# Moving one multiplication from VectorE to GpSimd, pooling the PSUM banks and reordering a four-layer kernel

## The reference

```
num_re = cumsum(p_w * cos(phi)); num_im = cumsum(p_w * sin(phi))
out_re = sum_m(s_re * qr + s_im * qi)
```

## Time and profile before

| what | value |
|---|---|
| median of three runs | 1407.12 us (1404.32, 1407.12, 1527.14) |
| profiled execution | span 1405.9 us; no other time of this execution is listed |
| granted TensorE clock, mean | 0.936 of full speed |
| busy share of the span, PE / DVE / ACT / POOL | 87% / 77% / 75% / 24% |
| HBM traffic | 71 GB/s over the span |

### The profile page before, as it was taken

How to read it: one execution, slowest core, us unless ns; L and a number is a source line. 1 busy time by engine, 2 the same in 40 slices (tenths; PEclk the granted TensorE clock), 3 DMA queues, 4 the chain that set the end, 5 groups by cost and what they waited for, 6 DMA issues and landing times.

```text
span 1405.9 us, 23146 instructions
## 1 busy us (share of the span) xinstructions
PE 1216.6 (87%) x8060; PEld 778.2 (55%) x8060; DVE 1089.1 (77%) x2259; ACT 1052.2 (75%) x2103; POOL 333.9 (24%) x317
## 2 busy tenths in 40 slices
PE   5889885999899988998799989999899988977347
PEld 2575653465556754675556755666566655534224
DVE  3683388788788979889788989898688988887830
ACT  4675788797959878797859888788949887458522
POOL 3944110520133102320124112310133110510101
PEclk9799996999999999999999999999999999998669
DMA  8504141514142123521333041523151140031100
GB/s 254 113 9 102 27 130 42 115 31 116 46 102 72 23 75 88 126 46 41 98 91 82 24 128 28 132 44 103 38 120 38 26 131 28 23 96 50 37 0 15
DMA packets 72084, 101.65 MB, mean 72 GB/s; under 512 B 10640, under 2 KB 44064, under 8 KB 71968
## 3 DMA queue, kind: packets, MB, share of 16 engines
q1 hardware_dynamic: 71968, 100.16, 27.3%
HBM read 74.44 MB, written 25.69 MB: 71 GB/s over the span
## 4 chain that ended last, share of the span: by engine, by line
PE 54%; DVE 16%; ACT 16%; issue 6%; POOL 5%; SPq 1%; DMA 1%; POOLq 0%; DVEq 0%; ACTq 0%
PE ps L873 19%; PE ps L883 15%; PE ps L956 5%; DVE work L1516 4%; ACT work L1203 4%; PE ps L1042 4%; DVE work L1439 3%; PE ps L974 3%; PE ps L948 3%; ACT work L1210 3%; DVE work L1507 2%; ACT xnd L1146 2%; DVE work L1525 2%; PE ps L865 1%; DVE work L1394 1%
## 5 line engine op out<-in xcount | busy, mean ns | idle before, releaser
L1516 DVE TENSOR_TENSOR_SCAN work<-work 128x512 f32<-128x512 f32 x256 | 313.1, 1255 | 39.5 <-ACT work L1270 37.8
L1203 ACT ACTIVATE work<-work 128x384 f32<-128x384 f32 (+3 forms) x512 | 264.4, 559 | 54.6 <-DVE work L1439 52.7
L1439 DVE CUSTOM_DVE_ANT_0 work<-ps,work 128x384 f32<-128x384 f32 (+3 forms) x512 | 228.0, 486 | 90.8 <-PE ps L948 87.0
L752 POOL TENSOR_TENSOR later_norms<-later_norms,singles 128x2 f32<-128x2 f32 x112 | 97.0, 867 | 768.9 <-ACT xnd L1146 465.4
L956 PE MATMUL ps<-ident,work 128*128 128x128 f32 x1280 | 203.4, 285 | 21.4 <-DVE work L1439 10.2
L956 PEld LDWEIGHTS ps<-ident,work 128*128 128x128 f32 x1280 | 151.8, 145 | 84.5 <-issue 35.3
L1210 ACT COPY work<-ps 128x512 f32<-128x512 f32 x300 | 169.9, 573 | 7.8 <-PE ps L956 7.3
L1525 DVE TENSOR_TENSOR work<-work 128x1024 f32<-128x1024 f32 x128 | 160.0, 1250 | 4.3
L948 PE MATMUL ps<-work 96*128 96x384 bf16 (+3 forms) x512 | 124.1, 310 | 38.7 <-ACT work L1210 32.1
L873 PE MATMUL ps<-led_xTd,wf 128*128 128x512 f32 x256 | 120.3, 621 | 3.9 <-issue 3.9
L873 PE MATMUL ps<-led_xTd,wfc 128*128 128x512 f32 x256 | 118.0, 596 | 0.0
(11 more groups left out here) (176 smaller groups left out, 1950.7 us busy)
## 6 DMA issues: line engine op xcount, KB each, us to landing
work<-values SPq DMA_DIRECT2D x64, 256.0 KB, 3.1
work<-ratios SPq DMA_DIRECT2D x64, 256.0 KB, 3.2
scratch<-work SPq DMA_DIRECT2D x32, 384.0 KB, 4.7
work<-scratch SPq DMA_DIRECT2D x64, 192.0 KB, 3.9
work<-scratch SPq DMA_DIRECT2D x64, 128.0 KB, 4.2
x_in<-x SPq DMA_DIRECT2D x8, 512.0 KB, 6.7
work<-scratch SPq DMA_DIRECT2D x64, 64.0 KB, 4.3
values<-work SPq DMA_DIRECT2D x16, 256.0 KB, 3.2
```

The costliest lines, as they stand in the source:

```text
L1203: i = s_.activation(part_of, part_of, ACT.Exp, scale=-1.0, bias=nmax[:, row:row + 1])
L1439: i = v_.tensor_tensor_reduce(sc[:, n % 4, at:at + nk], out_of(b, name)[:, at:at + nk], base_of(qt), -SCORE_SCALE, BIG, ALU.add, ALU.min, ...
L1516: v_.tensor_tensor_scan(ring[:, at, m, :], pwr[:, slot, :], ring[:, at, m, :], 0.0, ALU.mult, ALU.add).then_inc(*scanned.one)
```

## The change

- **Banks.** plan_banks takes the eight banks as one pool. A string BANKS of digits gives the bank of each PSUM use in the order of PE's list. PV and the gathers lose their own banks; PV is drained by ACT's copy as any other bank. The signal o_copied goes.
- **Token tiles.** out, fproj, oout and gproj are four items of one token tile each instead of one or two items; two tiles share a bank, and its signal is given after the second. The instructions are the same; other items can now stand between two tiles.
- **mix on POOL.** The 128 multiplications are issued by POOL, with the same operands and the same waits; PARTS moves "mix" from "dve" to "pool".
- **Orders.** All five MERGE strings are new.

What the new lists hold, counted from them: behind the second scan of a unit, VectorE's next item is at once another scan, frac or turn in 71 of 128 units; one or two other items stand between in 29; three or more in 28. For batches 1 to 5 together these are 37, 19 and 24; for batches 6 and 7 they are 23, 8 and 1. (Items that do nothing on VectorE are not counted.) On POOL, three mixes stand among the eight squares of batch 1's fc and two among those of each of batches 2 to 6; in batches 0 and 7 the squares stand together. On ACT, the four turns, folds 0 to 3, cos 0 to 2 and sin 0 and 1 of batch 7 now come before the two oystats of batch 6; before, three turns did and every fold, cos and sin stood behind them. On PE, the tail behind the last out has the same products and gathers as before. The gather 1 of batch 6 moves behind fc 7 of batch 7, and VectorE's gystats 0 of batch 6 moves from behind scan 11 of batch 7 to behind scan 27.

```diff
+def token_items(item, half):
+    return [(item, 2 * half), (item, 2 * half + 1)]
...
-    "dve": "stats ckv q qr k kr base S T OT sum fsum z weights ratio total rates turn frac scan mix gate silu "
+    "dve": "stats ckv q qr k kr base S T OT sum fsum z weights ratio total rates turn frac scan gate silu "
...
-    "pool": "stats q k ystats fstats fc fystats zstats oystats gstats gystats gsum ternary tables late",
+    "pool": "stats q k mix ystats fstats fc fystats zstats oystats gstats gystats gsum ternary tables late",
...
     "pool":
-        "a p a4 p8 a3 d2 a4 d15 a3 d2 a4 d16 a7 d18 a3 d4 a2 d a2 d17 a d4 a2 d2 a4 d16 a d4 a2 d2 a4 d20 a7 "
-        "d22 a2 d34",
+        "a2 p a3 p4 a4 d2 a3 d15 a m6 a3 m d2 m a3 d3 m d m d3 m d m3 d m2 d7 a m2 a m a2 m a2 d2 m a m d m d m "
...
+        "m d m6 d2 m3 d2 m9 d m2 d11 p4",
...
+BANKS = """
+0123450123450134250134250134201532045203420532405124305241024512405214032154032143201432041325401324
...
+"""
...
 def plan_banks():
+    place, uses, fills, banks = {}, [0] * 8, [0] * 8, iter("".join(BANKS.split()))
+    for chain, b, item, n in order_of("pe"):
+        for name in names_of(item, n) if chain != "p" else ():
+            k = int(next(banks))
+            uses[k] += 1
+            fills[k] += item not in ("PV", "gather")
+            place[b, name] = (k, uses[k], fills[k])
...
                     is_drained(pool, b, f"fc{n}")
                     g_.tensor_tensor(hid[:, n, :], hid[:, n, :], hid[:, n, :], ALU.mult).then_inc(*hid_sq.one)
+                if item == "mix":
+                    r, half = unit(n)
+                    both = ring[:, (COS_HALF, SIN_HALF)[half][r]]
+                    if n == 0 or n == RL:
+                        is_drained(pool, b, f"query{n // 2}")
+                        is_drained(pool, b, f"query{n // 2 + 1}")
+                    need(pool, scanned, b, 2 * (n + 1))
+                    g_.tensor_tensor(both, both, qc[:, half * MH:(half + 1) * MH], ALU.mult).then_inc(*mixed.one)
...
-            def tokens_out(b, tag, half, lhs, rhs, n_k):
+            def token_out(b, tag, tt, lhs, rhs, n_k):
+                name = f"{tag}{tt // 2}"
+                if tt % 2 == 0:
+                    may_fill(pe, b, name)
+                for j in range(n_k):
+                    i = mm(ps[:, bank(b, name), tt % 2 * D:(tt % 2 + 1) * D], lhs[:, j, tt * P:(tt + 1) * P],
+                           rhs[:, j, :], start=j == 0, stop=j == n_k - 1)
+                if tt % 2:
+                    i.then_inc(*fills(b, name))
...
                     if k == 0:
-                        need(pe, o_copied, b, hg)
+                        may_fill(pe, b, f"PV{hg}")
...
-                    s_.copy(osb, ps[:, PV, :]).then_inc(*o_copied.one)
+                    s_.copy(osb, out_of(b, f"PV{n // len(SUMS)}")).then_inc(*drains(b, f"PV{n // len(SUMS)}"))
...
                     if half == 0:
-                        may_fill(pe, b, f"mem{quad}")
+                        may_fill(pe, b, f"gather{quad}")
```

More of the change, by code:

```diff
@@ L85, in attention_items @@
             items += ["stats+", "centre+"] * after
-    items += ["attnT"] + ["norm+"] * after + ["out", ("ystats", 0), ("ystats", 1)] + ["xT+"] * after + [("sum", 0), ("sum", 1)]
+    items += ["attnT"] + ["norm+"] * after + token_items("out", 0) + [("ystats", 0)] + token_items("out", 1) + [("ystats", 1)]
+    items += ["xT+"] * after + [("sum", 0), ("sum", 1)]
     return steps(b, items)
+def token_items(item, half):
+    return [(item, 2 * half), (item, 2 * half + 1)]
 def first_dense_items(b):
-    return steps(b, [("fc", g) for g in range(HC)] + [("fproj", 0), ("fystats", 0), ("fsum", 0), ("zstats", 0), ("znorm", 0), ("fproj", 1),
-                     ("fystats", 1), ("zxT", 0), ("fsum", 1), ("zstats", 1), ("znorm", 1), ("zxT", 1), ("z", 2), "weights", ("z", 0), "ratio", ("z", 1), ("query", 0), ("query", 1), "total", "rates",
+    return steps(b, [("fc", g) for g in range(HC)] + token_items("fproj", 0) + [("fystats", 0), ("fsum", 0), ("zstats", 0), ("znorm", 0)] +
+                 token_items("fproj", 1) + [("fystats", 1), ("zxT", 0), ("fsum", 1), ("zstats", 1), ("znorm", 1), ("zxT", 1), ("z", 2), "weights", ("z", 0), "ratio", ("z", 1), ("query", 0), ("query", 1), "total", "rates",
                      ("query", 2), ("query", 3)])
 def second_dense_items(b):
-    return (steps(b, ["oout", ("oystats", 0), ("oystats", 1), ("osum", 0), ("osum", 1), ("gstats", 0), ("gstats", 1), ("gnorm", 0),
+    return (steps(b, token_items("oout", 0) + [("oystats", 0)] + token_items("oout", 1) + [("oystats", 1), ("osum", 0), ("osum", 1), ("gstats", 0), ("gstats", 1), ("gnorm", 0),
                        ("gxT", 0), ("gnorm", 1), ("gxT", 1)] + [("gc", g) for g in range(HC)]) + head_items(b + 2) +
-            steps(b, [("gproj", 0), ("gystats", 0), ("gsum", 0), ("gproj", 1), ("gystats", 1), ("gsum", 1)]))
+            steps(b, token_items("gproj", 0) + [("gystats", 0), ("gsum", 0)] + token_items("gproj", 1) + [("gystats", 1), ("gsum", 1)]))
 def head_items(b):
@@ L234, in merged @@
     return order
+def merged(engine):
+    return order_of(engine)
 def turn_on_act(b):
     return b in (0, B - 1)
-def plan_banks():
-    place, uses = {}, {}
-    def use(b, name, bank):
-        uses[bank] = uses.get(bank, 0) + 1
-        place[b, name] = (bank, uses[bank])
-    last = {"a": 2, "d": 6, "first": 2}
-    def names(item, n):
-        pairs = {"xT": "xT", "attnT": "aT", "out": "y", "oout": "oout"}
-        if item in pairs:
-            return [pairs[item] + "0", pairs[item] + "1"]
-        if item in ("ckv", "qr", "kr", "total"):
-            return [item]
-        if item in ("q", "k", "v", "base", "S", "T", "OT", "fxT", "fc", "fproj", "zxT", "gxT", "gc", "gproj"):
-            return [f"{item}{n}"]
-        if item == "query":
-            return [f"q_{n}"]
-        return [f"z{n}" if n < RH else "zs"] if item == "z" else []
-    for chain in "ad":
-        for b, item, n in chains()[chain]:
-            for name in names(item, n):
-                if chain == "a" and b == 0 and item in ("S", "T", "OT"):
-                    last["first"] = (last["first"] + 1) % 5
-                    use(b, name, (0, 1, 2, 4, 5)[last["first"]])
-                    continue
-                last[chain] = (last[chain] + 1) % 3 if chain == "a" else 4 + (last[chain] - 3) % 3
-                use(b, name, last[chain])
-    for b in range(B):
-        use(b, "mem0", 7), use(b, "mem1", 7)
-    return place, uses
@@ new lines, in names_of @@
+def names_of(item, n):
+    if item in ("xT", "attnT"):
+        return [item + "0", item + "1"]
+    if item in ("out", "fproj", "oout", "gproj", "gather"):
+        return [f"{item}{n // 2}"] * (n % 2 == 0)
+    if item == "PV":
+        return [f"PV{n // len(SUMS)}"] * (n % len(SUMS) == 0)
+    if item in ("ckv", "qr", "kr", "total"):
+        return [item]
+    if item in ("q", "k", "v", "base", "S", "T", "OT", "fxT", "fc", "zxT", "z", "query", "gxT", "gc"):
+        return [f"{item}{n}"]
+    return []
@@ L277 @@
+def plan_banks():
+    place, uses, fills, banks = {}, [0] * 8, [0] * 8, iter("".join(BANKS.split()))
[5 more added lines that the diff above has]
+            place[b, name] = (k, uses[k], fills[k])
+    assert next(banks, None) is None
+    return place, uses, fills
 class Signal:
@@ L440, in sandwich_kernel @@
         ps = ctx.enter_context(nc.psum_tensor("ps", [P, 8, 512], F32))
-        PV = 3
-        filled = {k: signal(f"bank{k}_filled", 0, 1, n) for k, n in bank_uses.items() if k != 7}
-        drained = {k: signal(f"bank{k}_drained", 0, 1, n) for k, n in bank_uses.items()}
+        filled = [signal(f"bank{k}_filled", 0, 1, n) for k, n in enumerate(bank_fills)]
+        drained = [signal(f"bank{k}_drained", 0, 1, n) for k, n in enumerate(bank_uses)]
         x_loaded = signal("x_loaded", 1, 16)
@@ L874, in product @@
                 i.then_inc(*fills(b, name))
-            def tokens_out(b, tag, half, lhs, rhs, n_k):
-                name = f"{tag}{half}"
-                may_fill(pe, b, name)
-                for t in range(2):
-                    tt = 2 * half + t
-                    for j in range(n_k):
-                        i = mm(ps[:, bank(b, name), t * D:(t + 1) * D], lhs[:, j, tt * P:(tt + 1) * P],
-                               rhs[:, j, :], start=j == 0, stop=j == n_k - 1)
-                i.then_inc(*fills(b, name))
+            def token_out(b, tag, tt, lhs, rhs, n_k):
[7 more added lines that the diff above has]
+                    i.then_inc(*fills(b, name))
             xa_c = [xTa[:, c, :] for c in range(DC)]
@@ L986, in do @@
                     is_drained(pe, b, "OT3")
-                    transposes(b, "aT", att)
+                    transposes(b, "attnT", att)
                 if item == "out":
@@ L1006, in do @@
                     need(pe, hid_sq, b, HC)
-                    tokens_out(b, "fproj", n, hid, wpr, HC)
+                    token_out(b, "fproj", n, hid, wpr, HC)
```

(14 more changed lines are left out.)

64 lines of the change are left out of this document (36 added, 28 removed), and 82 rows, old and new, of the table MERGE.

## The result

The changed kernel takes 1500.22 us (median of 4 runs, 1495.39 to 1505.07) against 1408.01 us (median of 4 runs) for the kernel before: a ratio of 1.0667, 95% interval 1.063 to 1.0703. The ratio compares fast runs alone and leaves out one slow run of the kernel before, 1527.14 us. The changed kernel is slower by 94 us where 1402 was forecast, and it lies outside the forecast range of 1346 to 1460.

What follows compares the result with a forecast made beforehand. PE was taken as the limit in the steady stage, with VectorE's time counting fully in the last 90 us. From 1407 us, banks -26, POOL's queue +8, the end +13 and steady stage 0 gave 1402 us, range 1346 to 1460.

Steps and rivals of the forecast that it cites:

- its own sign of being wrong: The forecast is wrong if the last mixer is shorter than before, or if PE's steady share falls.
- part 3: VectorE and POOL operations with two SBUF inputs block each other: 199 us against 146 given up; steady +21 costed at nothing.
- Parts 1 and 2: 128 mixes of 1.14 us, 146 us, leave VectorE; on POOL each takes 2.29 us, 293 us in all.
- Part 4: The end, batches 6 and 7: blocked scans against freed mixes, earlier waves and a later last mix, sum +13 us.
- Part 5: POOL's queue: rsqrt and squares wait behind mixes, mostly covered by attention, +8 us.
- Part 6: Banks, token tiles, orders: freer banks save half of PE's 51 us of bank waits, -26 us; token items 0.
- faster rival: Mixes mostly run beside reductions or idle stretches, so VectorE keeps its 1.14 us a unit: 1352 us, chance 0.28.
- slower rival: Mixes around the first FFN's squares on POOL delay fproj and the next mixer, +52 us: 1452 us, chance 0.30.

Runs made afterwards that it cites:

- experiments 7 and 8: Changed kernel with zero fills for the 71 mixes followed at once by scan, frac or turn: 1391.88 us; with fills for the 57 others instead: 1468.23 us.
- Experiment 6: Changed kernel with real POOL mixes in batches 0 to 5 and zero fills in batches 6 and 7: 1452.59 us.
- experiment 4: Kernel before, its banks, items and orders kept, with the mix alone moved to POOL: 1459.93 us; the same with zero fills for mixes: 1399.77 us.
- experiment 5: Changed kernel with real POOL mixes in batches 6 and 7 only and zero fills in the others: 1408.98 us.
- experiment 3: Changed kernel with only 16 of each mix's 1024 columns multiplied on POOL, the rest left out: 1346.0 us.
- experiment 11: Kernel before, own lists and mixes on VectorE, with only the eight banks in one pool and a token tile's two items side by side: 1388.81 us.
- experiment 2: Changed kernel with each mix replaced by two zero fills on POOL that write the same columns and read none: 1367.48 us.
- experiment 1: Changed kernel with each mix back on VectorE right behind its unit's second scan, all else kept: 1460.2 us.

## Why the prediction was wrong

The mechanism was named, its amount was over-estimated, and its own sign of being wrong came: PE's steady share fell. What failed is one step of part 3: "I cost it at nothing: VectorE is idle 122 of 865 us there and PE has attention work to do."

- **Parts 1 and 2 held.** The mix's 2.29 us measured 2.34 at the shortest and 2.54 in the median, since POOL's mixes wait for scans as well.
- **Part 3, the amount: right in kind, too large.** Forecast: 199 us of standing; VectorE near 1140 us busy. Measured: 153.8 us, 129.5 of them in the scans; VectorE busy 1108.8. The order of the placements was right too, with a unit followed at once by a scan dearer than one with something between. Both prices were too high: by VectorE's busy time the 71 units stood 123 us, 1.7 each instead of 2.16, and the 57 others 30 us, 0.5 each instead of 46 / 57 = 0.8 (experiments 7 and 8).
- **Part 3, the price, failed.** The steady stage's +21 us net was set to 0. Two errors are in it. The first is to take idle time for cover. VectorE's idle time lies where it waits for PE's scores and ACT's waves; a scan stands at other moments, ahead of the reduction that PE waits for next. Experiment 6 shows 108 us of standing in batches 0 to 5 (88 in scans) costing 86.5: the cover was a fifth, not all. The second is to net the blocks against the freed time. In the old lists the freed 146 us are worth 4.5 us and the standing 125 us cost 61 (experiment 4): the same microsecond of VectorE had two prices, by where it lies. The first paragraph of the forecast had said that work taken from VectorE is worth little in the steady stage; it was not said that work added there can cost most of its time. So even the 21 us that part 3 names for a lost cover are far too few.
- **Part 4, the end: near, in part by luck.** Forecast +13 us; the stretch behind the last PV copy measured +10, with a unit at 4.34 to 4.38 us against 4.5. But it took 60 us of standing in batches 6 and 7 where experiment 5 shows 45, and had no term for the slower gathers.
- **Part 5, POOL's queue: too small.** Forecast +8; experiment 3 against 2 shows 21 for fills of 1.93 us. PE's waits for squares did grow, to 9.5 us.
- **Part 6, banks: too large alone.** Forecast -26; experiment 11 shows -15.5 with the old lists. That all bank waits would go was more than expected; that normed rows are late next was named, and they took part of the gain.

So the 94 us are: -37 for all that the change does without the reads (experiment 2), within which banks and items alone give -15.5 and VectorE's freed time alone -4.5 in the old lists, and +131 for the reads. The split depends on the order of the steps: with the mixes still on VectorE the lists, banks and items make +54 (experiment 1), and the move on top of them another +40. Part 6 sets no price on the new orders by themselves; while VectorE keeps the mixes they have one. The faster rival's condition, scans that keep their 1.22 us, was made true by experiment 2, and gave 1367 against its 1352. The slower rival had the sign and much of the size, 1452, but the wrong place: it needed 52 us from squares that come late, and PE's whole wait for squares is 9.5 us. That the kernel without reads is faster than before does not speak against this rival, since its late scans go with the reads.

Open: why the new lists make a standing microsecond cost 0.85 of itself (131 for 154) and the old ones 0.49. That they leave less slack between VectorE and PE is likely, since their freed time is also worth more, (1.0385 - 0.9736) x 1407 = 91 of 146 us. Nearest to a test of the lists by themselves are experiments 1 and 11, which differ in the lists, the bank string made for them and the place of the mixes on VectorE: there the new lists are (1.0385 - 0.989) x 1407 = 70 us slower, while with fills, VectorE being free, lists, banks and items together are 33 us faster (experiments 2 and 4). This suggests that the new lists pay only while VectorE has time to spare, and that the reads take that time back. Whether lists found with the blocks in their costs would make the move pay was not tried.

## What to carry to other kernels

Before moving work to an idle engine, look in a timeline for what the two engines already do to each other when both read SBUF, count how often such instructions will stand next to each other, and price the standing at its full time unless a row shows what hides it: the idle share of a stage does not. Here it cost between half and all of itself. Time freed and time blocked on the same engine don't cancel, because each is worth what waits behind it at that moment. To price such a block, replace the instruction by one that keeps the engine, the order and the waits but not the reads.

## What was not expected of the hardware

A POOL fill of 1024 columns (0.965 us), which reads nothing, leaves VectorE's scans alone: their mean is 1256 ns beside 256 fills, 1253 in the kernel of experiment 11, whose mixes are on VectorE, and 1762 beside 128 multiplications. So it is not POOL's activity that stops a scan but POOL's reading of SBUF. The Trainium skill, page SBUF — State Buffer, section Who interferes with whom, says that a VectorE instruction with two SBUF inputs contends with a GpSimd instruction that reads SBUF and not with one that only writes it; these runs agree. And 16 columns of multiplication (median 378 ns) leave the mean scan at 1254 ns: so in these runs a hold cost by its length, not by its being there.
